# Graph convolutions on one core: TensorE and VectorE loops of two step groups instead of four, with rings of two one-hots and two PSUM banks

## The chip, the cores and the metric

The kernel runs on one core of one Trainium2 chip. The metric is the device time of one execution in microseconds (us). Three executions of the kernel before took 15028.1, 15060.8 and 15099.16 us; the median is 15060.8. The engines are named as in the profile: PE is TensorE (PEld its weight loads), DVE is VectorE, ACT is ScalarE, POOL is GpSimd, SP is SyncE.

## The reference, cut to what matters

Four message-passing layers run one after the other over the same graph of 12500 nodes and 200000 edges, sorted by destination. The change touches the last one, two graph convolutions:

```
def gcn_conv(x, src, dst, W, b, n_nodes):
    deg = segment_sum(ones, dst)
    dinv = where(deg > 0, rsqrt(maximum(deg, 1.0)), 0.0)
    norm = dinv[src] * dinv[dst]
    h = x @ W
    return segment_sum(h[src] * norm[:, None], dst) + b

h = relu(gcn_conv(x, src, dst, W1, b1, n))
out = gcn_conv(h, src, dst, W2, b2, n)
```

The kernel takes the multiplication by W out of the sum: it gathers rows of `dinv * x` by source node, sums them per destination node, and multiplies the sums by `dinv` and W afterwards.

## The kernel before

**Steps and groups.** Edges stand in tiles of 128, nodes in 98 windows of 128. A step is one edge tile with one node window that it touches; steps are taken in groups of G = 8, and there are 208 groups (S = 1664 steps). Edge rows are gathered in tiles of 8 x 128 edges: 196 such tiles for each convolution (TT = 49 turns of four).

**The gathers.** POOL runs `conv_tiles` (L699) over 16 ring slots (LONG = 16): eight indirect DMAs for each tile (L691), each of which brings 128 rows of 64 floats from `gcn_tab` into `g_ring`, a part of `tab`. Before tile h it waits for `free`, the semaphore g0_sums (g1_sums in the second convolution), to reach h + 1 (`tile_gathers`). VectorE raises that semaphore by AHEAD = 3 at the start (L1761), and TensorE by one with each group that it ends (L1146). So tile h waits for the end of group h - 3, counted from 0. Ring slots are handed back that way because a late group still needs tiles up to twelve behind. ACT (L801) copies the indices of the next tile when rows have landed, and its count is what TensorE takes as "landed".

**TensorE** runs `aggregate` (L1133). For group g it waits for the bank (`bank_free` >= g + 1), clears PSUM bank q = g mod 4 by a matmul with zeros (L1138), waits for the one-hots (`left_ready`), loads the places of the group's eight steps into registers (`load_steps`, L431 to L437), waits for the rows, and does eight matmuls (L1144), one-hot times gathered rows. An f32 matmul stands in the trace as two passes, so a group is 16 PE and 16 PEld entries of L1144.

**VectorE** runs `gcn` (L1757). Its loop takes the same groups. In iteration g it makes the one-hots of group g + 2 (eight tensor_scalar of L458, into `g_hot[(q + 2) % 4]`, two slots in `buf_a` and two in `buf_d`), reads the group's first window, waits for the sums of group g, and adds the PSUM bank to `acc_w` (L1773). Then it hands back the bank (L1775).

Each queue runs its own program in order; nothing else sets the order of the work. The other stages of the kernel (up to 10250 us) don't touch this code.

Of the kernel before, what the change touches and what calls it, by code (L numbers as in the profile page):

```python
# [34 lines left out]
ITER = S // PAIR  # L35
# [7 lines left out]
RING = 4  # L43
TURNS = S // G // RING
# [9 lines left out]
AHEAD = LONG - (W + G - 2) // G  # L54
# [21 lines left out]
def build(nc, x, src, dst, ea16, ea64, w_edge, b_edge, w_node, b_node,  # L76
          w_filter, b_filter, gamma_f, beta_f, w_core, b_core, gamma_c, beta_c,
          w_att, a_att, w1, b1, w2, b2, out):
    with ExitStack() as ctx:
# [31 lines left out]
        buf_a = sb("buf_a", [P, 2, G, 2 * D])  # L111
# [41 lines left out]
        g_ring = tab_flat[:, 0:LONG * G * D]  # L153
        g_rows = [g_ring[:, k * G * D:(k + 1) * G * D].rearrange("p (u f) -> p u f", f=D) for k in range(LONG)]
        g_places = tab_flat[0:1, PLACES_AT:PLACES_AT + S // G * GP].bitcast(I32)
        g_hot = [buf_a[:, 0, :, :], buf_a[:, 1, :, :], buf_d[:, 0, :, :], buf_d[:, 1, :, :]]
        gate_i = gate_s[:, :].bitcast(I32)
        l2_ring = tab_flat[:, 0:L2_RING * G * D2]
        l2_rows = [l2_ring[:, k * G * D2:(k + 1) * G * D2].rearrange("p (u f) -> p u f", f=D2) for k in range(L2_RING)]
# [296 lines left out]
        def one_hot_by_step(engine, to, g):  # L456
            for u in range(G):
                last = engine.tensor_scalar(to[:, u, :], iota[:, :], step_col(dst_s, g, u), None, ALU.is_equal)  # L458
            return last
# [467 lines left out]
        def _(pe):  # L927
# [203 lines left out]
                return last  # L1131

            def aggregate(left_ready, landed, free, done):  # L1133
                with pe.Fori(0, TURNS) as i:
                    for q in range(RING):
                        g = i * RING + q
                        pe.wait_ge(free, g + 1)
                        pe.matmul(ps[:, q, :].rearrange("p (k f) -> p k f", f=P), zero_b[:, :],  # L1138
                                  bc(ident_b[:, :].unsqueeze(1), [P, 4, P]), start=True, stop=False, skip_group_check=True)
                        pe.wait_ge(left_ready, g + 1)  # L1140
                        rel, at, needed = load_steps(g)
                        pe.wait_ge(landed, needed)
                        for u in range(G):
                            last = pe.matmul(ps_flat[:, bass.ds(rel[u] + q * 512, D)], g_hot[q][:, u, :], g_ring[:, bass.ds(at[u], D)],  # L1144
                                             start=False, stop=True, skip_group_check=True)
                        last.then_inc(done, 1)  # L1146
# [114 lines left out]
        def _(dve):  # L1261
# [495 lines left out]
            def gcn(conv, hot, outs, bank_free, order):  # L1757
                twice(twice_g, w12[:, conv, :])
                dve.memset(acc_w[:, :, :], 0.0).then_inc(order, 1)
                dve.sem_inc(bank_free, RING)  # L1760
                dve.sem_inc(outs, AHEAD)  # L1761
                for g in range(2):
                    one_hot_by_step(dve, g_hot[g], g).then_inc(hot, 1)
                with dve.Fori(0, TURNS) as i:
                    for q in range(RING):
                        g = i * RING + q
                        dve.wait_ge(outs, g + (AHEAD - 1))
                        one_hot_by_step(dve, g_hot[(q + 2) % RING], g + 2).then_inc(hot, 1)
                        w0 = load1(mybir.EngineType.DVE, win_s, g, W - 1)
                        dve.wait_ge(outs, g + (AHEAD + 1))  # L1770
                        a = acc_w[:, bass.ds(w0, G), 0:D]
                        dve.wait_ge(order, g + 1)
                        dve.tensor_tensor(a, a, ps[:, q, :].rearrange("p (k f) -> p k f", f=D), ALU.add).then_inc(order, 1)  # L1773
                        dve.wait_ge(order, g + 2)
                        dve.sem_inc(bank_free, 1)  # L1775
                for c in range(PAIRS):
                    dve.tensor_tensor(part_of(tab_d, c), part_of(sums_d, c), part_of(dinv_bc, c), ALU.mult).then_inc(s.gcn_scaled, 1)

# [43 lines left out]
```

## Time and profile before

| what | value |
|---|---|
| median of three executions | 15060.8 us |
| the profiled execution's own time | 15005.17 us |
| its span (first to last instruction) | 15003.3 us |
| busy share of the span: PE, PEld, DVE, ACT, POOL | 55%, 51%, 45%, 18%, 60% |
| the two convolutions in the span | about 10250 to 14950 us |
| gathers of the two convolutions (L691, `gcn_tab`) | 3136, 2986.0 us busy, mean 952 ns |

The page gives busy time by engine, the span in 40 slices, the DMA queues, the chain that ended last and the costliest groups of instructions. "Idle before" is the time in which an engine had nothing running just before a group's instructions, with what ended it. "issue" there is time in which the engine waited for nothing that the profile shows, and "remote" is a releaser that the profile could not put down to an instruction. Register, branch and semaphore instructions don't count as busy.

### The profile page before, as it was taken

What the parts mean: (1) busy time and instruction counts of PE and PEld (TensorE: products, weight loads), DVE (VectorE), ACT (ScalarE), POOL (GpSimd) and SP (SyncE); (2) the same over time, 40 slices, a digit from 0 to 9 for tenths busy, and PEclk for the clock granted to TensorE, in tenths of its full rate; (3) what the DMA queues carried; (4) which work ended last, traced back from release to release, by engine and by line L of the source; (5) the groups of instructions that cost most, each with busy time, mean ns of one, the idle gap of its engine ahead of it and who ended that gap; (6) DMA issues with size and microseconds to landing.
All of it is one profiled execution on the core that took longest, in us unless ns stands there. A gap on an engine that the chain in (4) does not pass through costs nothing.

```text
span 15003.3 us, 181666 instructions
## 1 busy us (share of the span) xinstructions
PE 8287.5 (55%) x46670; PEld 7635.5 (51%) x46671; DVE 6679.2 (45%) x13205; ACT 2744.9 (18%) x6542; POOL 9034.8 (60%) x8046
## 2 busy tenths in 40 slices
PE   5777777754555555578856555563333334333334
PEld 5777777754444444467745455463333333333333
DVE  6444444434444444479956556574222223222223
ACT  0111111101111111156633334341000000000000
POOL 3888888874555555510017777774666664666664
PEclk7666666667677777789967767675555555555555
DMA  5333333332333333333212222231111111111111
GB/s 91 18 18 18 18 18 18 18 50 80 91 91 92 91 91 91 91 100 99 98 49 69 64 66 71 63 79 31 23 23 23 23 23 26 23 23 23 23 23 23
DMA packets 851085, 769.36 MB, mean 51 GB/s; under 512 B 652784, under 2 KB 660804, under 8 KB 848965
## 3 DMA queue, kind: packets, MB, share of 16 engines
q0 software_dynamic: 446272, 333.87, 16.8%
q1 hardware_dynamic: 371597, 322.68, 6.8%
q10 hardware_dynamic: 33170, 112.27, 2.3%
q8 instruction: 21, 0.34, 0.0%
q14 instruction: 25, 0.20, 0.0%
HBM read 569.49 MB, written 197.82 MB: 51 GB/s over the span
## 4 chain that ended last, share of the span: by engine, by line
issue 23%; another core or an unknown queue 18%; PE 13%; DVE 12%; SPq 10%; POOL 10%; DMA 9%; DVEq 4%; ACT 0%; ACTq 0%; POOLq 0%
POOL lane_tab L667 8%; DMA lane_tab<-rows,idx 8%; SPq L562 7%; PE ps L1129 3%; PE ps L1144 3%; DVE buf_c L1519 2%; SPq L424 2%; DVE acc_w L1773 1%; DVEq L447 1%; DVEq L458 1%; PE ps L1232 1%; PE ps L1213 1%; PE ps L1168 1%; PE ps L1154 1%
## 5 line engine op out<-in xcount | busy, mean ns | idle before, releaser
L691 POOL DMA_INDIRECT tab<-gcn_tab,idx x3136 | 2986.0, 952 | 1718.5 <-issue 1148.2
L667 POOL DMA_INDIRECT lane_tab<-rows,idx x1664 | 2599.8, 1562 | 616.2 <-issue 613.5
L691 POOL DMA_INDIRECT tab<-att_tab,idx x1568 | 1762.5, 1124 | 1928.3 <-DVEq L1660 1330.1
L1144 PE MATMUL ps<-tab,buf_d 128*128 x3328 | 794.4, 387 | 2171.3 <-issue 2118.7
L1144 PEld LDWEIGHTS ps<-tab,buf_d 128*128 128x128 f32 x3328 | 782.0, 320 | 2283.8 <-issue 2283.7
L1773 DVE TENSOR_TENSOR acc_w<-acc_w,ps 128x512 f32 x416 | 286.3, 688 | 3422.0 <-remote 2957.1
L681 POOL DMA_INDIRECT buf_b<-src_tab,idx x832 | 834.2, 1003 | 802.5 <-DVEq L1522 339.5
L681 POOL DMA_INDIRECT acc_w<-src_tab,idx x832 | 840.0, 1010 | 654.9 <-DVEq L1522 399.9
L1103 PE MATMUL ps<-tab,buf_d 128*128 x3328 | 892.6, 361 | 354.5 <-DVEq L1523 331.7
L1043 PE MATMUL ps<-ident,srcg 128*128 128x128 f32 x3328 | 723.1, 405 | 656.2 <-DVE srcg L1406 653.5
L1144 PEld LDWEIGHTS ps<-tab,buf_a 128*128 128x128 f32 x3328 | 726.0, 330 | 652.9 <-issue 652.6
L1144 PE MATMUL ps<-tab,buf_a 128*128 x3328 | 762.8, 424 | 534.1 <-issue 446.3
L1043 PEld LDWEIGHTS ps<-ident,srcg 128*128 128x128 f32 x3328 | 669.3, 307 | 705.5 <-DVE srcg L1406 701.4
L1103 PEld LDWEIGHTS ps<-tab,buf_d 128*128 128x128 f32 x3328 | 738.7, 274 | 393.0 <-issue 392.5
L1104 PE MATMUL ps<-wte,buf_a 128*128 128x128 f32 x3328 | 858.2, 348 | 137.4 <-issue 136.8
L801 ACT ACTIVATE idx<-gate_s 128x8 int32 x392 | 81.8, 209 | 4427.2 <-DMA tab<-gcn_tab,idx 4427.2
L1060 PE MATMUL ps<-tab,buf_d 128*128 x3328 | 878.2, 355 | 0.0
L1213 PE MATMUL ps<-ident,tmp_c 128*128 128x128 f32 x3328 | 560.5, 333 | 392.7 <-issue 286.7
L1104 PEld LDWEIGHTS ps<-wte,buf_a 128*128 128x128 f32 x3328 | 722.1, 266 | 104.1 <-issue 104.0
L1232 PE MATMUL ps<-tab,buf_d 128*128 x3328 | 516.4, 319 | 435.0 <-issue 401.0
L1089 PE MATMUL ps<-ident_b,aux 128*128 128x128 bf16 x1680 | 234.0, 288 | 942.5 <-issue 790.2
L1213 PEld LDWEIGHTS ps<-ident,tmp_c 128*128 128x128 f32 x3328 | 536.0, 249 | 424.4 <-issue 411.9
(283 smaller groups left out, 17226.4 us busy)
## 6 DMA issues: line engine op xcount, KB each, us to landing
y_stash<-buf_c SPq DMA_DIRECT2D x208, 512.0 KB
tab<-y_stash SPq DMA_DIRECT2D x208, 512.0 KB, 3.3
aux<-in_edge_attr_dram SPq DMA_DIRECT2D x1696, 32.0 KB
aux<-dst_rows ACTq DMA_DIRECT2D x104, 512.0 KB
buf_b<-dst_rows ACTq DMA_DIRECT2D x104, 512.0 KB
tab<-gcn_tab,idx POOLq DMA_INDIRECT x3136
lane_tab<-rows,idx POOLq DMA_INDIRECT x1664
tab<-att_tab,idx POOLq DMA_INDIRECT x1568
```

Of the source, the lines that this page charges most:

```text
L562: sp.dma_start(ea_s[:, q, u, :], ea64[bass.ds(starts[u], P), :]).then_inc(e_in[q], 16)
L667: pool.indirect_dma_start(lane_tab[k][:, :], bass.IndirectOffsetOnAxis(ap=idx[:, b, u:u + 1], axis=0), rows[:, b, u, 0:D1], None, compute_ ...
L681: pool.indirect_dma_start(to[q][:, u, :], None, table[:, :], bass.IndirectOffsetOnAxis(ap=idx[:, q, u:u + 1], axis=0)).then_inc(rows_in[q] ...
L691: pool.indirect_dma_start(to[k][:, u, :], None, table[:, :], bass.IndirectOffsetOnAxis(ap=idx[:, k % RING, u:u + 1], axis=0)).then_inc(row ...
L1043: last = pe.matmul(region(8 * b + u, P), bc(srcg[:, b, u:u + 1], [P, P]), ident[:, :], start=True, stop=True)
L1060: last = pe.matmul(region(o, D), buf_d[:, b, u, :], window(tab, ws[u], D), start=True, stop=True)
L1103: pe.matmul(o, buf_d[:, b, u, :], window(tab, ws[u], P), start=True, stop=False)
L1104: last = pe.matmul(o, buf_a[:, b, u // 2, :], wte[:, u % 2, :], start=False, stop=True)
L1129: last = pe.matmul(ps_flat[:, bass.ds(rel[u] + bank * 512, n)], left[:, u, :], right[:, u, 0:n], start=False, stop=True, skip_group_check= ...
L1144: last = pe.matmul(ps_flat[:, bass.ds(rel[u] + q * 512, D)], g_hot[q][:, u, :], g_ring[:, bass.ds(at[u], D)], start=False, stop=True, skip ...
L1213: last = pe.matmul(region(u, P), bc(s_cols[:, q % 2, u:u + 1], [P, P]), ident[:, :], start=True, stop=True)
L1232: last = pe.matmul(ps_flat[:, bass.ds(rel[u] + bank * 512, D1)], l2_hot[q % 2][:, u, :], l2_ring[:, bass.ds(at[u], D1)], start=False, stop ...
```

## The change

TensorE and VectorE now turn over two groups in each pass of their loops, in ITER = 104 passes instead of TURNS = 52. There are two one-hot slots (both in `buf_a`) instead of four, and two PSUM banks (0 and 1) instead of four. VectorE gives TensorE two banks at the start instead of four. The one-hots of group g + 2 are made after the addition of group g, into the slot that group g has just left; their own wait for the sums of an earlier group is gone, since the addition has waited for more. POOL's gathers, AHEAD, ACT's index copies and the first two one-hots ahead of the loop stay as they are.

```
-        g_hot = [buf_a[:, 0, :, :], buf_a[:, 1, :, :], buf_d[:, 0, :, :], buf_d[:, 1, :, :]]
+        g_hot = [buf_a[:, 0, :, :], buf_a[:, 1, :, :]]
...
             def aggregate(left_ready, landed, free, done):
-                with pe.Fori(0, TURNS) as i:
-                    for q in range(RING):
-                        g = i * RING + q
+                with pe.Fori(0, ITER) as i:
+                    for q in range(2):
+                        g = i * 2 + q
                         pe.wait_ge(free, g + 1)
...
-                dve.sem_inc(bank_free, RING)
+                dve.sem_inc(bank_free, 2)
                 dve.sem_inc(outs, AHEAD)
                 for g in range(2):
                     one_hot_by_step(dve, g_hot[g], g).then_inc(hot, 1)
-                with dve.Fori(0, TURNS) as i:
-                    for q in range(RING):
-                        g = i * RING + q
-                        dve.wait_ge(outs, g + (AHEAD - 1))
-                        one_hot_by_step(dve, g_hot[(q + 2) % RING], g + 2).then_inc(hot, 1)
+                with dve.Fori(0, ITER) as i:
+                    for q in range(2):
+                        g = i * 2 + q
                         w0 = load1(mybir.EngineType.DVE, win_s, g, W - 1)
                         dve.wait_ge(outs, g + (AHEAD + 1))
...
                         dve.wait_ge(order, g + 2)
                         dve.sem_inc(bank_free, 1)
+                        one_hot_by_step(dve, g_hot[q], g + 2).then_inc(hot, 1)
```

VectorE's queue at the head of the loop of the first convolution, before: the end of the one-hots of group 2 and then the addition of group 0 (g0_sums counts TensorE's finished groups, g0_added the additions).

```order
L458 TENSOR_SCALAR buf_d<-iota,dst_s 128x128
L458 ISA
L458 TENSOR_SCALAR buf_d<-iota,dst_s 128x128
L447 ISA
L447 TENSOR_LOAD place_s
L1770 REGISTER_ALU
L1772 REGISTER_ALU [waits g0_sums]
L1773 ISA [waits g0_added]
L1773 TENSOR_TENSOR acc_w<-acc_w,ps 128x8x64
```

The same place now (the lines have moved up by two):

```order
L1764 ISA
L447 TENSOR_LOAD place_s
L1768 REGISTER_ALU
L1770 REGISTER_ALU [waits g0_sums]
L1771 ISA [waits g0_added]
L1771 TENSOR_TENSOR acc_w<-acc_w,ps 128x8x64
L1772 REGISTER_ALU
L458 ISA [waits g0_added]
L458 TENSOR_SCALAR buf_a<-iota,dst_s 128x128
```

The one-hots of group g + 2 stood ahead of the wait for the sums of group g; now they stand behind it and behind the addition, and go into `buf_a`.

TensorE's queue at the end of the second group of the loop, first convolution, now (before, the third group followed here, with its one-hots in `buf_d`, and the branch stood behind the fourth):

```order
L1144 ISA
L1144 MATMUL ps<-tab,buf_a 128x64
L1144 ISA
L1144 MATMUL ps<-tab,buf_a 128x64
L1134 REGISTER_ALU
L1134 COMPARE_AND_BRANCH
```

What TensorE does for one group is unchanged; the branch now comes every second group.

## Rows read from the trace of the kernel before

**Rows 1.** The page: span, and queues (name, kind: packets, MB, share).
```profile
span 15003.3 us, 181666 instructions
...
q8 instruction: 21, 0.34, 0.0%
q14 instruction: 25, 0.20, 0.0%
```

**Rows 2.** Windows of L691: stretches (us), POOL busy, gathers, PE clock, DMA share, GB/s.
```profile
9100.00:9200.00 100.00, 80.29 (x65) 0.88 0.34 90
9300.00:9400.00 100.00, 75.91 (x80) 0.50 0.18 27
10319.95:12519.85 2199.90, 1462.53 (x1536) 0.50 0.13 23
12658.30:14858.60 2200.30, 1462.52 (x1536) 0.50 0.13 23
```

**Rows 3.** Waits of POOL in 10310:12519: line, releaser, us in total, times, longest.
```profile
POOL tab L691 <- issue: 453.7, 1488, 0.3
POOL tab L691 <- remote: 283.2, 48, 6.1
```

**Rows 4.** Timeline of POOL, one stall: start us, us, instruction, idle before.
```profile
11504.70 0.95 POOL L691 DMA_INDIRECT tab<-gcn_tab,idx  x1 [0.31 <-issue]
11511.60 0.95 POOL L691 DMA_INDIRECT tab<-gcn_tab,idx  x1 [5.95 <-remote]
```

**Rows 5.** Timeline of PE weight loads, the same stall and after it.
```profile
11508.65 0.29 PEld L1144 LDWEIGHTS ps<-tab,buf_d 128*128 128x128 f32 x1 [2.51 <-issue]
11510.76 2.00 PEld L1144 LDWEIGHTS ps<-tab,buf_d 128*128 128x128 f32 x9 [1.82 <-issue]
...
11515.61 3.48 PEld L1144 LDWEIGHTS ps<-tab,buf_a 128*128 128x128 f32 x16 [2.83 <-issue]
...
11521.34 3.49 PEld L1144 LDWEIGHTS ps<-tab,buf_a 128*128 128x128 f32 x16 [2.21 <-issue]
...
11527.09 3.27 PEld L1144 LDWEIGHTS ps<-tab,buf_d 128*128 128x128 f32 x15 [2.24 <-issue]
11530.71 0.29 PEld L1144 LDWEIGHTS ps<-tab,buf_d 128*128 128x128 f32 x1 [0.34 <-issue]
```

**Rows 6.** Timeline of DVE, the same stall and after it.
```profile
11510.97 0.69 DVE L1773 TENSOR_TENSOR acc_w<-acc_w,ps 128x512 f32 x1 [26.50 <-remote]
11511.92 1.72 DVE L458 TENSOR_SCALAR buf_a<-iota,dst_s 128x128 f32<-128x128 f32 x8 [0.26 <-DVE acc_w L1773]
11513.64 0.69 DVE L1773 TENSOR_TENSOR acc_w<-acc_w,ps 128x512 f32 x1
...
11526.02 0.69 DVE L1773 TENSOR_TENSOR acc_w<-acc_w,ps 128x512 f32 x1 [6.73 <-PE ps L1144]
```

**Rows 7.** Timeline of PE weight loads, the start of the first convolution.
```profile
10296.39 3.49 PEld L1144 LDWEIGHTS ps<-tab,buf_a 128*128 128x128 f32 x16 [6.43 <-issue]
```

**Rows 8.** Timeline, another layer (L681 gathers): end of a run of gathers.
```profile
5425.16 0.94 POOL L681 DMA_INDIRECT acc_w<-src_tab,idx  x1 [0.30 <-issue]
...
5427.00 0.10 PEld L1089 LDWEIGHTS ps<-ident_b,aux 128*128 128x128 bf16 x1 [1.29 <-issue]
...
5428.41 0.34 PEld L1089 LDWEIGHTS ps<-ident_b,aux 128*128 128x128 bf16 x4 [1.31 <-issue]
```

**Rows 9.** Timelines of POOL and PE weight loads, attention layer: end of a run.
```profile
9406.92 0.95 POOL L691 DMA_INDIRECT tab<-att_tab,idx  x1 [0.30 <-issue]
9423.25 0.95 POOL L691 DMA_INDIRECT tab<-att_tab,idx  x1 [15.39 <-remote]
...
9422.20 0.50 PEld L1220 LDWEIGHTS ps<-ident,buf_a 128*128 128x128 f32 x3 [1.92 <-issue]
```

**Rows 10.** Timelines of POOL and DVE, the end of the first convolution.
```profile
12513.01 0.94 POOL L691 DMA_INDIRECT tab<-gcn_tab,idx  x1 [0.30 <-issue]
...
12519.20 0.69 DVE L1773 TENSOR_TENSOR acc_w<-acc_w,ps 128x512 f32 x1 [26.46 <-remote]
...
12586.39 0.69 DVE L1773 TENSOR_TENSOR acc_w<-acc_w,ps 128x512 f32 x1 [3.19 <-PE ps L1144]
12612.89 0.94 POOL L691 DMA_INDIRECT tab<-gcn_tab,idx  x1 [98.93 <-issue]
```

## The prediction, made before the changed kernel was run

> **What bounds the convolutions.** I read the busy shares first, then POOL's gathers by stretch, POOL's waits, and last the timelines of POOL, PE and DVE around one wait. The reader is to see a gather queue that runs at its own pace and stops on a strict beat.
>
> POOL issues 1536 gathers in 2199.90 us of the first convolution and in 2200.30 us of the second, with 1462.5 us busy in each [rows 2]. That is 2199.9 / 48 = 45.83 us for 32 gathers, or four tiles; 11.46 us a tile. In between it stops 48 times, for 283.2 us in all, up to 6.1 us each [rows 3]: 5.9 us. So a beat is 40 us of gathers at a pitch of 1.25 us, and a stop of 5.9. Two such convolutions hold 96 stops, 96 x 5.9 = 566 us, which is all that a change of TensorE's and VectorE's loops could win here.
>
> What does POOL wait for? By the code, for the end of group h - 3. Yet TensorE is quick: a group is 3.5 us of weight loads and starts 5.7 us after the one before (11515.61, 11521.34, 11527.09) [rows 5], against 10 us for a tile of gathers. The stop has another shape. Before it TensorE issues one pass every 2.8 us (idle 2.51 before each), and at 11510.76 nine passes go at once [rows 5]. VectorE, which had been waiting 26.5 us, starts its addition at 11510.97 [rows 6]. POOL goes on at 11511.60 [rows 4]. Three engines come free within 0.9 us, 5.1 us after POOL's last gather ended (11504.70 + 0.95 = 11505.65). And the addition at 11526.02 waited 6.73 us for a group whose weight loads had ended at about 11519.1 [rows 5, 6]. So the other engines are slowed down while POOL issues gathers back to back, TensorE's counts reach VectorE and POOL late, and all is released some time after POOL stops. POOL stops because the count it waits for is among those held back.
>
> It is the same at the start of the convolution, where TensorE does its group in 3.49 us after 6.43 us of idle time [rows 7] and so is not short of anything: the beat there is in the same 48 stops.
>
> How long does the release take? In the convolution 5.1 us after a run of 40 us [rows 4, 5]. In another layer, after a run of 15 gathers (19 us), TensorE is free at 5428.41, 2.3 us after the end of the last gather at 5426.10 [rows 8]. In the attention layer POOL issues 80 gathers in 100 us, again at 1.25 us each [rows 2], and after that TensorE comes free at 9422.20, 14.3 us after 9407.87 [rows 9]. So 5.1 / 40 = 0.13, 2.3 / 19 = 0.12, and 14.3 over somewhat more than 100 us is about 0.13: the release takes about 0.13 of the run ahead of it. Where other transfers are busy, POOL needs 100 / 65 = 1.54 us a gather [rows 2]. POOL's mean pace of 45.83 / 32 = 1.43 us is thus nearly a property of the gathers, however the stops are cut.
>
> **The change, part by part.** It alters how far TensorE can go ahead of the count that VectorE has seen. Before, with the sums of groups up to g - 1 seen, the one-hots of group g + 2 existed and banks were free for three more groups; TensorE could do g, g + 1 and g + 2. Now the one-hots of g + 2 need the sum of g seen, so it can do g and g + 1 only. In the stretch in which counts are held back TensorE was half through its third group (nine of 16 passes left at the release) [rows 5]; now it idles there. That half group is made up after the release.
>
> *Instructions.* The eight one-hots, the addition, the clearing matmul and the eight matmuls of a group stay. Loops branch 52 times more on two engines in each convolution. I cost that at nothing: TensorE needs 5.7 us of each 11.46 and VectorE 0.69 + 1.72 us and small gaps, about 2.7 [rows 5, 6]. If that cover were gone, a branch of half a microsecond would be 104 x 0.5 = 52 us at most.
>
> *The new chain.* Sum of g seen, addition and one-hots until 11513.64 from 11510.97, 2.7 us; then TensorE's register loads, 2.2 us (its idle time before a group), and its matmuls, 3.7 us [rows 5, 6]: 8.6 us for two groups in flight, 4.3 us a group. TensorE's own pitch of 5.7 us is longer, so the chain sets nothing while counts pass at once.
>
> *The beat.* At a release POOL used to find three counts (two held back, and the half-done group 2 us later) and got a fourth 15 us on, which let it issue four tiles. Now it finds two. The third group ends 8.6 us on, and the next 5.7 us behind it, at 14.3 us, about when counts begin to be held. So I expect three tiles in a run, sometimes two, sometimes four. With three: 24 gathers, 29.75 us to the end of the last, 0.13 x 29.75 = 3.9 us to the release, and 0.84 us until the first gather, as now (11510.76 to 11511.60): 34.5 us, 11.49 a tile. With two: 19.7 + 2.6 + 0.84 = 23.1 us, 11.57 a tile. Against 11.46 that is +0.03 and +0.11, times 392 tiles +12 and +43 us. I take +18, nearer to the first.
>
> The cost of a stop after a 30 us run isn't in the trace. Its bounds are the rows on both sides: 0.12 of the run, +0, and the whole 5.9 us of now, (30 + 5.9) / 3 = 11.97 a tile, +0.51 x 392 = +200 us; below nothing, a stop could vanish if counts were held less with an idler TensorE, to 10 us a tile. I take the proportional value since three layers agree on it.
>
> *The end of a convolution.* From the first addition after the last release to the last one it is 12586.39 - 12519.20 = 67.2 us [rows 10], with TensorE at its own pitch and no gathers. The first group then ended 2 us after the release; now it ends 8.6 us after it. That is +6 us in each convolution, +12 in all. The stretch from there to the next convolution's first gather at 12612.89 does not change.
>
> Sum: 18 + 12 = +30 us. The profiled execution took 15005 us, which makes 15035; it lies 56 us below the median of the runs shown, so against that the forecast is 15,090 us, +0.2%. A run of this kernel tells about 0.5% (75 us) from no change, so this counts as no change.
>
> **Rivals.**
>
> *Faster: the shorter loop is what TensorE lacked.* One could read the slow passes as a loop too long to be kept near the engine: they come once in a turn of four groups, at the same place. If halving the loop ended them, POOL would never be held, and the 96 stops go: 15,060 - 566 = 14,495 us. Against it: VectorE is let go in the same 0.3 us as TensorE, from a wait of its own; other layers with other loops show the same release just behind POOL's last gather [rows 8, 9]; and the queues that bring instructions moved 21 and 25 packets in the whole span [rows 1], against 104 turns of this loop alone. I give it 1 in 10.
> The Trainium skill, page "Runtime: NRT & Kernel Launch", section "Instruction fetch mechanics", states the rule for this rival: instructions come in blocks of 16 KiB, and a taken branch to a target outside the window held on the chip costs a fetch by DMA. By that rule a loop of half the size could only gain; the packets counted in this trace don't show such fetches.
>
> *Slower: a stop costs the same however short the run.* This is the shallow ring's price: two groups ahead instead of three, so POOL is stopped more often, at 5.9 us each. It decides from the point where TensorE's second count after a release comes too late to be seen before the run's end. With three tiles a run 11.97 us a tile, +200 + 12: 15,270 us. With two tiles (20 + 5.9) / 2 = 12.95 a tile, +584 + 12: 15,655 us. For it: the stops of now are alike to 0.3 us, and only one run length occurs here; and the one-hots now hang on counts that are held back. Against it: the 2.3 and 14.3 us of the other layers [rows 8, 9]. I give 0.24 to the first size and 0.12 to the second.
>
> *The change does nothing to the beat.* Runs stay at four tiles, since with TensorE idler the count that is now too late is let through earlier. Then only the ends count: +12, 15,075 us. It is within the forecast's own case.
>
> *A small gain*: the release comes at less than 0.13 of the run now that TensorE issues less while counts are held. At 0.10 of a 30 us run it is 3.0 instead of 3.9 us, 0.3 us a tile, 118 us: 14,970 us. No row shows a share under 0.12; I give it 0.04.
>
> **Chances and range.** No change (forecast and unchanged beat) 0.50; slower by over 0.5% 0.24 + 0.12 = 0.36; faster by over 0.5% 0.10 + 0.04 = 0.14. The likeliest case's own range is 15,030 to 15,130. The range to hold 8 in 10 runs from 14,990, which leaves out the large gain, to 15,350, which takes in the slower rival's first size and leaves out its second.
>
> **What would show it.** The forecast: POOL's waits in a convolution are more than 48, each shorter than 5.9 us, with a sum within 40 us of 283; 1.43 us a gather stays; PE idles while the counts are held and has no half group; 73 us or so from the last release to the last addition. The fetch rival: no PE passes at 2.8 us any more, hardly a wait of POOL. The slower rival: about 64 or 96 waits of the old length. Wrong altogether if POOL's pace between stops departs from 1.25 us, or if TensorE's count is missing because the group wasn't done, which would show as POOL waits ended by PE right behind a matmul of L1144.

## The result and the profile after

The kernel after took 15156.33 us (median of 20 runs, 15064.14 to 15184.69), the kernel before 15063.74 us on the same chips (20 runs, 15005.35 to 15128.38). The ratio is 1.0045, with a 95% interval of 1.0029 to 1.0061: slower by 0.45%, about 68 us. The forecast was 15,090 us, the range 14,990 to 15,350, and the likeliest case "within 0.5%". The measured time is in the range, but above the 15,030 to 15,130 us that the likeliest case was given.

The profiled execution of after took 15176.89 us. From its page:

```profile
span 15175.1 us, 182290 instructions
...
q8 instruction: 20, 0.33, 0.0%
q14 instruction: 24, 0.20, 0.0%
```

The last two lines are the queues that bring instructions. They moved as little as in [rows 1], though the loops now branch twice as often.

The two profiled executions lie 171.8 us apart, and only part of that is the change. From POOL's timelines I took the first and the last gather of each convolution. All numbers are us, and they add up to the span's end:

| stretch | before | after | difference |
|---|---|---|---|
| first instruction to first gather of convolution 1 | 10274.6 | 10386.9 | +112.3 |
| first to last gather, convolution 1 | 2238.5 | 2254.8 | +16.3 |
| from there to the first gather of convolution 2 | 99.9 | 114.1 | +14.2 |
| first to last gather, convolution 2 | 2238.8 | 2254.8 | +16.0 |
| from there to the end | 151.6 | 164.3 | +12.7 |

The changed part costs 59 us. The 112 us ahead of it are in code that the change does not touch. 87 of them are the pause of POOL ahead of convolution 1, which is 127 us in the one and 214 us in the other (from the start of the last gather of the attention layer to the first of the convolution). In the later runs, none of which touches that code, it is 115 to 166 us on one chip and 203 to 217 us on the two others, with the rings of before as with those of after. So single times of this kernel differ by 100 us for no reason of the change. Below I compare stretches of the convolutions, where the two convolutions of most runs agree within 1 us (4 us in ahead1), and times only where there are several rounds.

**The beat.** POOL's waits in most of convolution 1 (line, releaser: us in total, times, longest), which answer to [rows 3]:

```profile
POOL tab L691 <- issue: 436.9, 1433, 0.3
POOL tab L691 <- remote: 301.9, 67, 5.0
POOL tab L691 <- PE ps L1144: 4.3, 14, 0.3
```

Four of the 67 are the usual 0.3 us between gathers. The other 63 are stops, of 4.8 us on average, 301 us in all. A whole convolution has 64 stops and 306 us, where it had 48 of 5.9 us and 283. POOL's busy time and gathers in a stretch that holds whole beats (the view and the columns are those of [rows 2]):

```profile
10466.90:12612.80 2145.90, 1415.30 (x1488) 0.50 0.12 23
```

POOL stops every 24 gathers here: 1488 / 24 = 62 beats of 34.61 us, three tiles each, 11.54 us a tile. Before, 32 gathers took 45.83 us, 11.46 a tile [rows 2]. One such beat of POOL (start us, us, instruction, idle time before):

```profile
11505.27 0.95 POOL L691 DMA_INDIRECT tab<-gcn_tab,idx  x1 [4.86 <-remote]
...
11534.27 0.95 POOL L691 DMA_INDIRECT tab<-gcn_tab,idx  x1 [0.30 <-issue]
11539.92 0.94 POOL L691 DMA_INDIRECT tab<-gcn_tab,idx  x1 [4.70 <-remote]
```

TensorE's weight loads in the same beat (L1138 clears a bank, L1144 is the group):

```profile
11505.52 0.10 PEld L1138 LDWEIGHTS ps<-ident_b,zero_b 128*128 128x128 bf16 x1 [10.59 <-DVEq L1773]
11509.34 3.49 PEld L1144 LDWEIGHTS ps<-tab,buf_a 128*128 128x128 f32 x16 [3.72 <-issue]
...
11515.08 3.48 PEld L1144 LDWEIGHTS ps<-tab,buf_a 128*128 128x128 f32 x16 [2.21 <-issue]
...
11521.26 3.49 PEld L1144 LDWEIGHTS ps<-tab,buf_a 128*128 128x128 f32 x16 [2.67 <-issue]
11540.07 0.10 PEld L1138 LDWEIGHTS ps<-ident_b,zero_b 128*128 128x128 bf16 x1 [15.33 <-DVEq L1773]
```

And VectorE (L1771 is the addition, L458 the one-hots, now behind it):

```profile
11504.72 0.69 DVE L1771 TENSOR_TENSOR acc_w<-acc_w,ps 128x512 f32 x1 [17.93 <-remote]
11505.66 1.66 DVE L458 TENSOR_SCALAR buf_a<-iota,dst_s 128x128 f32<-128x128 f32 x8 [0.25 <-DVE acc_w L1771]
11507.30 0.69 DVE L1771 TENSOR_TENSOR acc_w<-acc_w,ps 128x512 f32 x1
...
11514.01 0.69 DVE L1771 TENSOR_TENSOR acc_w<-acc_w,ps 128x512 f32 x1 [4.11 <-PE ps L1144]
...
11539.28 0.69 DVE L1771 TENSOR_TENSOR acc_w<-acc_w,ps 128x512 f32 x1 [22.67 <-remote]
```

TensorE does three whole groups after a release, three counts pass, POOL issues three tiles. The groups of 11515.08 and 11521.26 are done by 11525, yet VectorE adds the first of them at 11539.28, when POOL has been still for 4 us. TensorE meanwhile idles 15.33 us for want of a bank; there are no slow passes any more, which before were the half group of [rows 5].

Not every count is held. ACT copies the indices of the next tile when all rows of a tile have landed (start us, us, instruction, idle before; the kernel before, in the run of gathers that ends in [rows 4]):

```profile
11497.23 0.21 ACT L801 ACTIVATE idx<-gate_s 128x8 int32 x1 [9.77 <-DMA tab<-gcn_tab,idx]
11507.23 0.21 ACT L801 ACTIVATE idx<-gate_s 128x8 int32 x1 [9.79 <-DMA tab<-gcn_tab,idx]
```

The copies come 10.0 us apart, at POOL's own pitch, and the last one 2.5 us after the start of the run's last gather (11504.70). So the rows have landed and ACT has seen them 3.5 us ahead of the release at 11510.76. The rows themselves don't lag behind; what is held are the counts that TensorE raises, and TensorE's passes.

**The end of a convolution**, which answers to [rows 10]: first POOL, then VectorE.

```profile
12641.73 0.94 POOL L691 DMA_INDIRECT tab<-gcn_tab,idx  x1 [0.30 <-issue]
12755.88 0.95 POOL L691 DMA_INDIRECT tab<-gcn_tab,idx  x1 [113.21 <-issue]
```

```profile
12646.83 0.69 DVE L1771 TENSOR_TENSOR acc_w<-acc_w,ps 128x512 f32 x1 [20.37 <-remote]
...
12657.90 0.69 DVE L1771 TENSOR_TENSOR acc_w<-acc_w,ps 128x512 f32 x1 [5.59 <-PE ps L1144]
...
12661.72 0.69 DVE L1771 TENSOR_TENSOR acc_w<-acc_w,ps 128x512 f32 x1 [1.22 <-PE ps L1144]
...
12726.94 0.69 DVE L1771 TENSOR_TENSOR acc_w<-acc_w,ps 128x512 f32 x1 [3.04 <-PE ps L1144]
12727.88 1.66 DVE L458 TENSOR_SCALAR buf_a<-iota,dst_s 128x128 f32<-128x128 f32 x8 [0.25 <-DVE acc_w L1771]
12729.45 7.10 DVE L1776 TENSOR_TENSOR tab<-acc_w,mx 128x896 f32<-128x896 f32 x7
```

Both kernels have 15 additions left at the last release. They take 80.1 us from the first to the last (12646.83 to 12726.94), against 67.2 [rows 10].

TensorE's register loads in this stretch (L432 is the load in `load_steps`; duration in ns: shortest, median, longest):

```profile
L432 PEldq TENSOR_LOAD <-tab x13: 1363/4034/4042, 12649.6 to 12718.6; - x13
```

One load in four takes 1.36 us and the others 4.03 us. In the kernel before they take the same.

### The profile page after: what moved, and what is told of

The parts are those of the page before. It is cut to its first block, busy times and chain, and to the rows that moved or that the text cites. A ratio compares the mean times of both kernels' runs of the same rounds, so it can differ in the third digit from the quotient of the medians.

```text
span 15175.1 us, 182290 instructions
## 1 busy us (share of the span) xinstructions
PE 8316.0 (55%) x46670; PEld 7626.2 (50%) x46671; DVE 6686.3 (44%) x13205; ACT 2744.1 (18%) x6542; POOL 9013.6 (59%) x8046
## 4 chain that ended last, share of the span: by engine, by line
another core or an unknown queue 22%; issue 21%; POOL 18%; PE 11%; SPq 10%; DVE 9%; DMA 7%; DVEq 1%; ACT 0%; POOLq 0%; ACTq 0%
POOL lane_tab L667 9%; POOL tab L691 9%; SPq L562 7%; DMA lane_tab<-rows,idx 7%; PE ps L1129 3%; PE ps L1144 3%; DVE buf_a L458 2%; SPq L424 2%; DVE buf_c L1519 2%; DVE acc_w L1771 1%; PE ps L1168 1%; PE ps L1154 1%; PE ps L1018 1%; DVE acc_w L1525 1%
## 5 line engine op out<-in xcount | busy, mean ns | idle before, releaser
L691 POOL DMA_INDIRECT tab<-gcn_tab,idx x3136 | 2982.1, 951 | 1855.5 <-issue 1231.9
L691 POOL DMA_INDIRECT tab<-att_tab,idx x1568 | 1745.3, 1113 | 1915.7 <-DVEq L1660 1320.8
L1144 PE MATMUL ps<-tab,buf_a 128*128 x6656 | 1518.9, 423 | 1427.8 <-issue 1348.7
L1144 PEld LDWEIGHTS ps<-tab,buf_a 128*128 128x128 f32 x6656 | 1457.0, 330 | 1632.0 <-issue 1627.4
L1771 DVE TENSOR_TENSOR acc_w<-acc_w,ps 128x512 f32 x416 | 286.6, 689 | 3571.6 <-remote 3046.5
L681 POOL DMA_INDIRECT buf_b<-src_tab,idx x832 | 835.0, 1004 | 854.2 <-DVEq L1522 352.9
L681 POOL DMA_INDIRECT acc_w<-src_tab,idx x832 | 839.9, 1010 | 659.2 <-DVEq L1522 404.2
L1138 PE MATMUL ps<-ident_b,zero_b 128*128 128x512 bf16 x416 | 259.5, 624 | 1621.5 <-DVEq L1773 1517.5
L1103 PE MATMUL ps<-tab,buf_d 128*128 x3328 | 886.4, 359 | 354.7 <-DVEq L1523 338.1
L1103 PEld LDWEIGHTS ps<-tab,buf_d 128*128 128x128 f32 x3328 | 733.4, 272 | 392.3 <-issue 392.0
L1104 PE MATMUL ps<-wte,buf_a 128*128 128x128 f32 x3328 | 850.6, 345 | 131.5 <-issue 131.4
L1138 PEld LDWEIGHTS ps<-ident_b,zero_b 128*128 128x128 bf16 x416 | 82.1, 197 | 1651.3 <-DVEq L1773 1542.0
L1060 PE MATMUL ps<-tab,buf_d 128*128 x3328 | 878.9, 356 | 0.0
L1232 PE MATMUL ps<-tab,buf_d 128*128 x3328 | 517.8, 320 | 482.1 <-issue 428.9
L458 DVE TENSOR_SCALAR buf_a<-iota,dst_s 128x128 f32<-128x128 f32 x3360 | 720.7, 305 | 103.7 <-DVE acc_w L1771 81.5
```

The source lines that it names most:

```text
L681: pool.indirect_dma_start(to[q][:, u, :], None, table[:, :], bass.IndirectOffsetOnAxis(ap=idx[:, q, u:u + 1], axis=0)).then_inc(rows_in[q] ...
L691: pool.indirect_dma_start(to[k][:, u, :], None, table[:, :], bass.IndirectOffsetOnAxis(ap=idx[:, k % RING, u:u + 1], axis=0)).then_inc(row ...
L1060: last = pe.matmul(region(o, D), buf_d[:, b, u, :], window(tab, ws[u], D), start=True, stop=True)
L1103: pe.matmul(o, buf_d[:, b, u, :], window(tab, ws[u], P), start=True, stop=False)
L1104: last = pe.matmul(o, buf_a[:, b, u // 2, :], wte[:, u % 2, :], start=False, stop=True)
L1232: last = pe.matmul(ps_flat[:, bass.ds(rel[u] + bank * 512, D1)], l2_hot[q % 2][:, u, :], l2_ring[:, bass.ds(at[u], D1)], start=False, stop ...
```

## The experiments

Edits are against the kernel before unless it is said. "Its before" is one run of the kernel before on the same chip. The first four kernels ran on one chip, the next four on another, the last three on a third; the beats of the chips differ by up to 0.5% (outside its last tiles late8 is the kernel before and late8_after the one after, and their beats are 46.04 and 34.75 us for 45.83 and 34.61). Only the last three kernels ran more than once; the time of each other kernel, and of its before, is a single execution, and shows nothing by itself. In the tables "1" and "2" are the lengths of the two convolutions (first to last gather), "between" and "end" the stretches behind them, all in us; the beat is the median time from the start of a run of gathers to the start of the next.

### Is it the loop's length?

**body4**: the kernel after, with two one-hots, two banks and its order, but loops of four groups again.

```
-                with pe.Fori(0, ITER) as i:
-                    for q in range(2):
-                        g = i * 2 + q
+                with pe.Fori(0, TURNS) as i:
+                    for q in range(RING):
+                        g = i * RING + q
...
-                        one_hot_by_step(dve, g_hot[q], g + 2).then_inc(hot, 1)
+                        one_hot_by_step(dve, g_hot[q % 2], g + 2).then_inc(hot, 1)
```

> The changed kernel's rings of two and its order (one-hots behind the addition), but loop bodies of four groups again. Theory of the depth (the count of TensorE is held back while POOL issues gathers back to back, and the ring of two lets TensorE finish only two groups ahead of the count): as the changed kernel, gathers of a convolution 2255 us from first to last, stops of 4.8 us after 24 gathers. Rival, the length of the loop body: the body decides, so as the kernel before, 2239 us and stops of 5.9 us after 32 gathers.

**body8**: the kernel before with loops of eight groups, 26 turns.

```
-                with pe.Fori(0, TURNS) as i:
-                    for q in range(RING):
-                        g = i * RING + q
+                with pe.Fori(0, TURNS // 2) as i:
+                    for q in range(2 * RING):
+                        g = i * (2 * RING) + q
```

> The kernel before (rings of four, one-hots ahead of the addition) with loop bodies of eight groups, 26 turns. Depth theory: no change, 2239 us for a convolution's gathers, 32 gathers and 5.9 us stops. Rival, the length of the loop body (instructions fetched in a turn): slow passes of TensorE grow with a body twice as long, stops longer than 5.9 us or more of them, 2300 us or more.

| | us (its before) | 1 | between | 2 | end | gathers in a run, beat |
|---|---|---|---|---|---|---|
| body4 | 15264.26 (15269.86) | 2265.6 | 112.9 | 2264.6 | 162.4 | 24, 34.76 |
| body8 | 15245.43 (15269.86) | 2249.6 | 99.9 | 2248.7 | 151.6 | 32, 46.05 |

POOL's waits of one beat in body4, and then in body8:

```profile
11511.05 0.94 POOL L691 DMA_INDIRECT tab<-gcn_tab,idx  x1 [4.92 <-remote]
...
11545.83 0.94 POOL L691 DMA_INDIRECT tab<-gcn_tab,idx  x1 [4.97 <-remote]
```

```profile
11507.09 0.95 POOL L691 DMA_INDIRECT tab<-gcn_tab,idx  x1 [5.84 <-remote]
...
11553.15 0.94 POOL L691 DMA_INDIRECT tab<-gcn_tab,idx  x1 [6.05 <-remote]
```

body4 has the runs and the ends of after, body8 those of before. body4 has the two stretches behind the convolutions within 2 us of those of after, body8 has those of before to the tenth. The number of groups in a turn doesn't matter; the effect is in the rings and the order. Both runs came as expected, and the fetch rival falls.

### Which ring?

**banks2**: two PSUM banks, but four one-hots, made ahead of the addition as before.

```
-                        pe.matmul(ps[:, q, :].rearrange("p (k f) -> p k f", f=P), zero_b[:, :],
+                        pe.matmul(ps[:, q % 2, :].rearrange("p (k f) -> p k f", f=P), zero_b[:, :],
...
-                dve.sem_inc(bank_free, RING)
+                dve.sem_inc(bank_free, 2)
```

> The kernel before with two PSUM banks instead of four; four one-hot slots, made ahead of the addition. Depth theory: two banks alone already let TensorE finish only two groups ahead of the count that VectorE has seen, so runs of 24 gathers, stops of 4.8 us, 2255 us a convolution. Rival, the late one-hots are what costs: as before, 2239 us.

**hots2**: two one-hot slots filled behind the addition, but four banks.

```
-                        dve.wait_ge(outs, g + (AHEAD - 1))
-                        one_hot_by_step(dve, g_hot[(q + 2) % RING], g + 2).then_inc(hot, 1)
...
+                        one_hot_by_step(dve, g_hot[q % 2], g + 2).then_inc(hot, 1)
```

> The kernel before with the one-hots behind the addition in two slots; four PSUM banks, bodies of four groups. Depth theory: the one-hots alone limit TensorE to two groups ahead as well, so again runs of 24 gathers, stops of 4.8 us, 2255 us. Rival, the banks are what costs: as before, 2239 us.

| | us (its before) | 1 | between | 2 | end | gathers in a run, beat |
|---|---|---|---|---|---|---|
| banks2 | 15231.42 (15269.86) | 2264.2 | 104.3 | 2264.6 | 154.7 | 24, 34.75 |
| hots2 | 15305.83 (15269.86) | 2263.8 | 112.5 | 2264.6 | 163.8 | 24, 34.75 |

Either limit alone lets TensorE go only two groups ahead of the counts that VectorE has seen, and either alone makes the runs of 24. Against body8 on the same chip the convolutions are 14 to 16 us longer in both. Of the cost behind them, 11 to 13 us in body4, banks2 has 3 to 4 and hots2 all of it. So the one-hots behind the addition account for the ends by themselves, and two banks add nothing once they are there, though alone they cost a third.

### What sets the length of a run?

**ahead2** and **ahead1**: POOL may go 2 or 1 tiles ahead of the counts instead of 3.

```
-AHEAD = LONG - (W + G - 2) // G
+AHEAD = 2
```

> The kernel before with AHEAD = 2 instead of 3: POOL may issue one tile less ahead of TensorE's count. Everything else, rings of four included, stays. Theory of the proportional release (other engines come free 0.13 of a run after POOL stops): runs of 24 gathers, stops of 4.8 us, a beat of 34.6 us, about 2255 us from the first to the last gather of a convolution, as with the changed kernel. Rival, a stop costs the same however short the run: 5.9 us after 24 gathers, 2350 us.

> The kernel before with AHEAD = 1. Proportional release: runs of 16 gathers (19.8 us), release 2.6 us later, stop about 3.4 us, a beat of 23.4 us or 11.7 a tile, about 2290 us from first to last gather, unless the awaited group is not done yet. Rival, fixed stop of 5.9 us: 12.97 a tile, 2540 us.

| | us (its before) | 1 | between | 2 | end | gathers in a run (runs), beat |
|---|---|---|---|---|---|---|
| ahead2 | 15033.04 (15077.96) | 2243.3 | 91.2 | 2243.4 | 141.5 | 32 (88), 45.85; 16 (14), 23.30 |
| ahead1 | 15138.40 (15077.96) | 2322.8 | 93.2 | 2327.0 | 131.4 | 32 (77), 45.86; 16 (14), 23.34; 8 (33), 16.15 |

(Left out are 15 runs of other lengths in ahead1 and four of 24 in ahead2.)

Waits in ahead2:

```profile
11517.50 0.94 POOL L691 DMA_INDIRECT tab<-gcn_tab,idx  x1 [6.13 <-remote]
...
11563.40 0.94 POOL L691 DMA_INDIRECT tab<-gcn_tab,idx  x1 [6.13 <-remote]
```

Both expectations failed: neither 24 nor 16 gathers is the usual run. Most of a convolution has runs of 32 with AHEAD at 2 and at 1. There a run is as long as the number of counts that pass in a beat, which is what the rings set.

The allowance does set the run at the start of each convolution. In ahead2 the first 17 tiles go in one run of 24 gathers and seven of 16. In ahead1 the first 16 tiles go one by one, then come runs of 16, and the runs are of 32 for good from tile 36 in the first convolution and 51 in the second. A convolution has 208 groups for 196 tiles, so the later a group, the further its tiles lie behind its number; that this loosens POOL's wait as it goes on fits, and was not tested.

The runs of eight in ahead1 are of another kind. Of POOL's waits in its first convolution (from 10300 us on), those that TensorE's matmuls ended:

```profile
POOL tab L691 <- PE ps L1144: 90.1, 14, 6.9
```

Their stop is 6.4 us, and ends when TensorE has done the group of the tile that just landed: work that isn't done yet, and not a count that is held.

The offset also shows at the end: one tile less ahead means less to make up behind the last gather (13 additions instead of 15), 9 to 10 us less in each of the two last stretches of ahead2.

### What is a stop made of?

**pause**: after each tile POOL waits until that tile's rows have landed, so a run is eight gathers.

```
+                pool.wait_ge(rows_in[k % RING], (i * (LONG // RING) + k // RING) * (G * 16) + (TURNS_BEFORE[2 + conv] + 1) * (G * 16))
+                pool.sem_inc(s.passed, 1)
```

> The kernel before, in which POOL waits after each tile of a convolution until its eight gathers have landed (about 2 us after the last was issued). Proportional release: 2 us after 10 us of gathers is more than the 1.3 us that a release takes, so counts are never held for long, TensorE's passes at 2.8 us and POOL's stops for the count go, a tile costs 10 + 2 = 12 us or a little less, 2330 us a convolution. Rival, the release needs a stop of its own of about 5 us: passes at 2.8 us remain, the stops of 5.9 us come on top of the pauses, 2650 us.

**half_rows**: each gather of the convolutions brings 64 rows instead of 128. The other half of the rows is left out.

```
+                    pool.indirect_dma_start(to[k][0:P // 2, u, :], None, table[:, :],
+                                            bass.IndirectOffsetOnAxis(ap=idx[0:P // 2, k % RING, u:u + 1], axis=0)).then_inc(rows_in[k % RING], 16)
```

> The kernel before with convolution gathers of 64 rows instead of 128; the rows of the other half are left out (stale values are summed in their place). If what holds the counts back builds up with the descriptors of the gathers, the release after POOL stops comes after about half the share (0.065 of the run) or POOL's pitch falls below 1.25 us; if it goes by gather instructions, the pitch stays at 1.25 us with the stop at 5.9 us and 2239 us a convolution.

| | us (its before) | 1 | between | 2 | end | gathers in a run, beat |
|---|---|---|---|---|---|---|
| pause | 15239.83 (15077.96) | 2417.9 | 36.7 | 2417.4 | 87.0 | 8, 12.20 |
| half_rows | 15050.70 (15077.96) | 2245.1 | 102.6 | 2245.6 | 153.1 | 32, 45.80 |

POOL and then TensorE in pause:

```profile
11514.62 0.94 POOL L691 DMA_INDIRECT tab<-gcn_tab,idx  x1 [2.42 <-ACT idx L803]
```

```profile
11514.07 3.49 PEld L1146 LDWEIGHTS ps<-tab,buf_a 128*128 128x128 f32 x16 [8.61 <-issue]
...
11526.31 3.49 PEld L1146 LDWEIGHTS ps<-tab,buf_d 128*128 128x128 f32 x16 [8.72 <-issue]
```

Nothing is held any more in pause: each group follows its tile, 12.2 us apart. Over a whole convolution a tile costs more than that, 0.92 us above before and not 0.75 (2417.9 against 2238.5 us): every 96 gathers POOL stops for another 1.86 us, which the profile puts down to nothing. The expectation, 2330 us, was too low in both parts. And POOL's wait in half_rows, then its windows row (columns as in [rows 2]):

```profile
11535.32 0.90 POOL L703 DMA_INDIRECT tab<-gcn_tab,idx  x1 [0.30 <-issue]
11543.57 0.90 POOL L703 DMA_INDIRECT tab<-gcn_tab,idx  x1 [7.34 <-remote]
```

```profile
10700.00:12400.00 1700.00, 1075.45 (x1184) 0.50 0.06 11
```

With half the rows (11 GB/s instead of 23) POOL issues a little faster, at 1.21 us a gather (1075.45 / 1184 = 0.91 busy, 0.30 idle), its run ends 1.3 us earlier, and the stop is 7.3 us instead of 5.9: the beat is 45.80 us, the same. Neither expected case came, since the pitch and the stop both changed and their sum did not. So the pace goes by the gather instructions and not by their rows, and the stop is what is left when POOL has run ahead of that pace.

The beats whose stop ends in a held count lie close to one line. From before and after, (45.83 - 34.61) / 8 = 1.40 us a gather, and 34.61 - 24 x 1.4025 = 0.95 us that come once a stop. It gives 23.4 us for 16 gathers (ahead2 23.30, ahead1 23.34). For eight it gives 12.2; pause has 12.20, but its stop is the wait for the landing, so that says nothing of the line, and the eight of ahead1, with a wait for TensorE's work, are off it at 16.15. The same from body8 and body4 is 1.41 and 0.9 us, and from ahead2's own two lengths 1.41 and 0.75. TensorE's slow passes show the same pace. In [rows 5] the one at 11508.65 comes 2.8 us after the one before, twice 1.40, though POOL's last gather ended 3 us earlier.

### Can the held time be kept out of the ends?

**late8**: the kernel before, with pause's wait in the last 12 tiles of each convolution only. **late8_after**: the same in the kernel after.

```
-                with pool.Fori(0, LT) as i:
+                with pool.Fori(0, LT - 1) as i:
...
+                for k in range(LONG):
+                    conv_tiles(conv, LT - 1, k, indices, free, k >= SETTLE)
...
-                    conv_tiles(conv, LT, k, indices, free)
+                    conv_tiles(conv, LT, k, indices, free, True)
```

> The kernel before, in which POOL waits for the landing of each of the last twelve tiles of a convolution (8 of the last turn of sixteen and the rest of 4) before it issues the next. Theory, TensorE is behind at a convolution's end only because its counts and instructions are held while gathers are issued back to back: in twelve tiles at 12.2 us TensorE, at 5.7 us a group, makes up its ten groups, so the stretch from the last gather of the first convolution to the first of the second falls from 99.9 to about 37 us, for 12 x 0.76 = 9 us more of gathers: 54 us less in each convolution, 108 us in all, 0.7% faster. Rival, the end is TensorE's own pace whatever POOL does: 99.9 us stay and the time grows by 18 us.

> The changed kernel with the same twelve waits of POOL. If the changed kernel's loss has two parts, 16 us of beat and 14 us at the end of each convolution, then the second goes and about 16 us of the first stays: 2264 us from first to last gather against 2247, the stretch between the convolutions about 37 us in both, 0.2% slower than the same waits on the kernel before.

**early_load**: the kernel before, with TensorE's register loads ahead of the clearing matmul and its waits.

```
                with pe.Fori(0, TURNS) as i:
                    for q in range(RING):
                        g = i * RING + q
+                        rel, at, needed = load_steps(g)
                        pe.wait_ge(free, g + 1)
...
                        pe.wait_ge(left_ready, g + 1)
-                        rel, at, needed = load_steps(g)
```

> The kernel before, in which TensorE loads a group's places into registers ahead of the clearing matmul and of its waits for bank and one-hots. Theory: POOL's gathers set the beat, so first to last gather stays at 2239 us; at the end of a convolution, where TensorE runs at its own 5.7 us a group, 1.5 us of the 2.2 us before a group may go under the matmuls of the group before: 99.9 falls to about 82 us, 0.2% faster in all. Rival, more groups in the free stretch of a beat let POOL run longer: runs of 40 gathers; by 1.41 us a gather of service that is no gain either.

These three ran in 5 rounds each; the kernel before beside them took 15250.4 us (23 runs).

| | us, runs | ratio to before, 95% | 1 | between | 2 | end |
|---|---|---|---|---|---|---|
| late8 | 15142.61, 6 | 0.9939 [0.9919, 0.996] | 2261.2 | 36.3 | 2260.3 | 86.8 |
| late8_after | 15197.85, 12 | 0.9966 [0.995, 0.9981] | 2274.9 | 42.9 | 2275.0 | 93.0 |
| early_load | 15253.25, 12 | 1.0 [0.9983, 1.0016] | 2246.1 | 99.6 | 2246.5 | 150.9 |

TensorE at the end of convolution 1 in late8, then POOL:

```profile
12748.34 3.49 PEld L1150 LDWEIGHTS ps<-tab,buf_d 128*128 128x128 f32 x16 [8.63 <-issue]
...
12763.25 3.49 PEld L1150 LDWEIGHTS ps<-tab,buf_d 128*128 128x128 f32 x16 [11.39 <-issue]
```

```profile
12757.64 0.94 POOL L692 DMA_INDIRECT tab<-gcn_tab,idx  x1 [0.30 <-issue]
12793.93 0.94 POOL L692 DMA_INDIRECT tab<-gcn_tab,idx  x1 [35.34 <-issue]
```

With the landing waits TensorE has caught up when the last gather is issued: one group is left instead of 12 and more, and POOL's pause between the convolutions is 35.34 us instead of 98.93 [rows 10]. late8 spends 14 to 15 us in each convolution, where 9 were expected (against early_load, whose beats are those of before), and saves 63 to 64 us behind each: 98 us by the stretches, 108 by the medians. It beats the kernel before by 0.6%, and with it the one after, which is slower than before. The shallow rings still cost it 14 to 15 us a convolution and 6 to 7 us an end (late8_after), where no cost at the ends was expected.

early_load gains nothing, where 0.2% was expected. TensorE's idle time moved, and did not shrink: (start us, us, idle before)

```profile
12766.16 3.49 PEld L1145 LDWEIGHTS ps<-tab,buf_a 128*128 128x128 f32 x16
12771.78 0.10 PEld L1140 LDWEIGHTS ps<-ident_b,zero_b 128*128 128x128 bf16 x1 [2.14 <-issue]
12772.06 3.48 PEld L1145 LDWEIGHTS ps<-tab,buf_d 128*128 128x128 f32 x16 [0.17 <-issue]
```

The 2.1 us now stand ahead of the clearing matmul instead of behind it, and the pitch of such a pair of groups is 5.9 us, where [rows 5] have 5.7. So the loads take their 4.03 us from TensorE's own queue, and cost the same wherever they stand in it.

## Why the prediction was right, and where it was mis-sized

The forecast case is the one that came: no change by the 0.5% bound, slightly slower, by the mechanism named. Luck has a part in the first: the change is 0.45%, its interval reaches to 0.61%, and the time is 66 us above the forecast and outside the likeliest case's own range. Two of its terms were too small, by about 14 and 15 us, which add up to 59 instead of 30; the 9 us from there to the 68 measured lie outside the convolutions or in the noise.

- *The release* was called proportional to the run, 0.13 of it. Held: 24 gathers, a stop of 4.7 to 4.9 us where 3.9 + 0.84 = 4.74 was forecast, a beat of 34.61 for 34.5. The slower rival needed stops of 5.9 us; none in this stretch is longer than 5.0. half_rows shows that the fraction itself is not the law: it is what is left of about 1.40 us a gather when POOL issues at 1.25, and it grows when POOL issues faster.
- *Three tiles a run*: held, and more strictly than forecast ("sometimes two, sometimes four"). But for one run of 32 in each convolution, all are of 24. TensorE's lead was the right cause, as banks2 and hots2 show; each of the two ring limits suffices.
- *The beat term*, mis-sized: +18 was taken, +32 measured (16.3 + 16.0). The step that failed is the small number under it: 11.49 us a tile against 11.457, where 11.537 was measured. 0.080 x 392 = 31 us. A tenth of a microsecond in a beat counts, since what remains of the two costs is the fixed part: 0.95 us a stop, with 64 - 48 = 16 stops more in each convolution, 32 x 0.95 = 30 us. The prediction had that part, as 0.84 us until the first gather, but took the release of a 30 us run from a fraction known to two digits: run, release and restart came to 34.46 us, where 34.61 was measured.
- *The end term*, mis-sized: +12 was taken, +27 measured (14.2 + 12.7). From the first to the fourth addition it takes 14.9 us (12646.83 to 12661.72) and took 8.5 before, +6.4 where +6 was forecast, but the step under it was wrong. The new chain was put at 8.6 us for two groups in flight, with 2.2 us for the register loads, read from TensorE's idle time before a group. That is only the part of a load that no matmuls cover. In the new order the load waits for the one-hots and takes its whole 4.03 us. From the addition at 12646.83 to the third at 12657.90 it is 11.07 us. The 11 additions from the fourth to the last take 65.2 us, 5.93 each, where they took 58.7, 5.34 each: +6.5 us. I had written that the chain "sets nothing" since it is shorter than TensorE's pitch. Of the mean that still holds: 11.07 us, or 8.4 with the short load, make 5.2 us a group as an estimate, against 5.34. But TensorE's pitch alternates (one group in four, the one with the short load, starts 3.5 us after the one before). Two neighbouring pitches of the additions, 3.8 and 5.4 us, made 9.2 us before. Now a group with a long load is added at least 11.07 us after the group two places ahead of it, and the pitches are 3.8, 7.3, 6.3 and 5.7 us. At 8.6 us the chain would have fitted under the 9.2. And "the stretch from there to the next convolution's first gather does not change" was wrong by 2.4 us (28.9 for 26.5), of which 1.66 are the one-hots that now stand behind the last addition (L458 at 12727.88), for a group that does not exist. The release, 1.1 us earlier after the shorter run, takes that off again: 6.4 + 6.5 + 2.4 - 1.1 = 14.2, as measured. hots2 has this whole end cost, banks2 a third of it.
- *Instructions at nothing*: held. body4 and body8 show it. So did the verdict on the fetch rival. The Trainium skill's page "Runtime: NRT & Kernel Launch", section "Instruction fetch mechanics", has a taken branch outside the fetched window cost a DMA; here the instruction queues moved 20 to 22 and 24 to 27 packets in a span with hundreds of such turns, at two, four and eight groups a turn.
- *The signs*: more and shorter waits with a sum within 40 us of 283 (64, 306 us) and an idle TensorE without a half group came. The 73 us from the last release to the last addition did not; it was 80.1.
- *Unforeseen*: how little POOL's allowance counts. I expected shorter runs of ahead2 and ahead1 throughout; they came only at the start of each convolution.

What stays open: what it is that goes at 1.40 us a gather, and by what way it holds TensorE's passes and the counts that VectorE and POOL wait for. It is not the landing of the rows, which ACT sees 2.5 us after a tile's last gather all through a run. That TensorE and VectorE are held by the same thing as POOL's count is argued from their common release. The 0.95 us once a stop are fitted, and not seen as one wait.

## What to carry to other kernels

When several engines come free in the same microsecond just behind a run of gathers, look whether the work that they wait for is long done. If it is, the wait belongs to the gathers: count the time per gather over a whole beat, and expect a change of the rings to move stops about rather than to remove them. Ring depth then costs little in the middle (32 stops more, 30 us in 4500) and about as much at the two ends (27 us in 280), where the held back work is made up with no gathers beside it; a few landing waits ahead of such an end bought four times what they cost. When a change puts a step behind a new wait, price it by its own duration in the trace, not by the idle time it left while other work covered it. And a chain that is shorter than the mean pitch of the engine it follows can still cost, if that pitch is uneven.

## What the runs showed of the hardware that I had not expected

- Indirect gathers issued back to back (a pitch of 1.25 us) cost about 1.40 us each over a whole beat, whether they bring 128 rows or 64 (beats of 45.83 and 45.80 us for 32). Their rows land at POOL's own pitch all the same.
- During such a run TensorE's counts reach VectorE and POOL late, by 20 us in the beat shown of after (weight loads done at 11518.6, addition at 11539.28), while the landing counts reach ACT 2.5 us after a tile's last gather.
- A landing wait after every eight gathers ends the holding of other engines altogether. It makes the beat of a tile 0.75 us longer (12.20 against 11.46; 0.92 over a convolution), and TensorE's groups start at once.
- TensorE's register load for a group took 4.03 us in three groups of four and 1.36 us in the fourth at the end of a convolution, ahead of the clearing matmul (early_load) as behind the wait for the one-hots.
- The same untouched pause of POOL ahead of convolution 1 was 115 to 166 us long in the runs on one chip and 203 to 217 us on two others, a larger difference than anything that this change did.
